# One-hot columns of a gather on TensorE: one wide compare of two tiles, or a compare per tile with a number per partition

## The reference

```python
for _ in range(2):                                   # the two passes that matter here
    edge_input = concatenate([h[src], h[dst], edge_attr_32], axis=-1)
    m_ij = relu(edge_input @ We1 + be1) @ We2 + be2
    h = h + segment_sum(m_ij, dst, num_segments=3125)
x = layernorm(x + (h + bias))
# third stage: out = segment_sum((x @ weight.T)[src] * norm, dst); relu; + x
x = layernorm(x + gcn(x))
```

## Time and profile before

| what | value |
|---|---|
| median of 3 runs | 2765.25 us (2763.64 to 2766.93) |
| profiled execution | 2764.02 us |
| its span, first to last instruction | 2762.2 us |
| TensorE (PE) busy | 2262.0 us, 82% |
| GpSimd (POOL) busy | 2012.3 us, 73% |
| VectorE (DVE) busy | 1467.6 us, 53% |
| ScalarE (ACT) busy | 703.4 us, 25% |
| mean granted TensorE clock | 0.882 |

### The profile page before, as it was taken

The page is one execution under the profiler, slowest core; times in us unless marked ns, Lnnn a source line. Parts: engine busy times, 40 slices in busy tenths (PEclk is TensorE's granted clock), DMA queues, the critical chain, the costliest instruction groups (busy, mean ns, idle before and its releaser), DMA issues.

```text
span 2762.2 us, 51738 instructions
## 1 busy us (share of the span) xinstructions
PE 2262.0 (82%) x15194; PEld 1711.8 (62%) x15384; DVE 1467.6 (53%) x3610; ACT 703.4 (25%) x1927; POOL 2012.3 (73%) x1765
## 2 busy tenths in 40 slices
PE   2798888888888888878788788888888868998986
PEld 2565656656566657555555555555555658888986
DVE  2755555554555554354444444444444368988885
ACT  2111111111111111111111111111111147877874
POOL 3677777777777777287887877777877737766763
PEclk8899999999989997589898999999898868999997
DMA  5333333333333334223333333333333321111111
GB/s 121 88 95 95 93 89 95 90 90 96 85 96 97 92 92 115 78 78 90 88 90 89 94 91 89 93 88 96 85 94 96 91 58 51 51 48 50 51 47 46
DMA packets 181877, 231.86 MB, mean 84 GB/s; under 512 B 75000, under 2 KB 133231, under 8 KB 181620
## 3 DMA queue, kind: packets, MB, share of 16 engines
q0 software_dynamic: 56000, 114.80, 15.7%
q1 hardware_dynamic: 118580, 111.47, 15.3%
q10 hardware_dynamic: 7168, 4.09, 0.5%
HBM read 220.06 MB, written 10.12 MB: 83 GB/s over the span
## 4 chain that ended last, share of the span: by engine, by line
POOL 47%; issue 31%; PE 10%; DVE 6%; DMA 3%; ACT 1%; DVEq 1%; POOLq 1%; SPq 0%; ACTq 0%
POOL gat L540 47%; PE ps L719 3%; PE ps L709 2%; PE ps L610 2%; DMA gat<-dst_row 1%; DVE msg L1282 1%; PE ps L797 1%; DVE khots L1277 1%; DMA gat<-z_dram,idx 1%; DMA cbase_dram<-cint 1%; PE ps L660 1%; DVE xTs L1279 1%; PE ps L793 1%; DMA dbc<-dst_row 1%; PE ps L628 0%
## 5 line engine op out<-in xcount | busy, mean ns | idle before, releaser
L540 POOL DMA_INDIRECT gat<-p_dram,idx x1422 | 1677.5, 1180 | 501.6 <-issue 430.8
L660 PE MATMUL ps<-node_a,x 128*128 128x512 bf16 x2210 | 779.7, 431 | 315.8 <-DVE node_a L1227 313.2
L660 PEld LDWEIGHTS ps<-node_a,x 128*128 128x128 bf16 x2400 | 247.2, 109 | 603.3 <-DVE node_a L1227 291.7
L1247 DVE TENSOR_TENSOR msg<-ps,gat 128x512 f32<-128x512 f32 (+1 forms) x404 | 250.9, 622 | 517.7 <-DMA gat<-p_dram,idx 500.4
L660 PE MATMUL ps<-node_a,adj 128*128 128x512 bf16 x1200 | 511.7, 426 | 0.0
L540 POOL DMA_INDIRECT gat<-z_dram,idx x328 | 322.0, 982 | 167.4 <-issue 98.3
L600 PEld LDWEIGHTS ps<-rhs,lhs 96*128 96x128 f32 x3232 | 408.2, 199 | 57.0 <-DVE lhs L1187 24.9
L600 PE MATMUL ps<-rhs,lhs 96*128 96x128 f32 x3232 | 412.0, 282 | 28.1 <-DMA rhs<-q_dram 21.8
L610 PE MATMUL ps<-hot,msg 128*128 128x64 f32 x3232 | 411.5, 282 | 12.8 <-ACT msg L902 12.8
L1187 DVE TENSOR_SCALAR lhs<-dbc,base_p 64x1024 f32<-64x1024 int32 x202 | 156.4, 774 | 486.1 <-DMA dbc<-dst_row 448.7
L610 PEld LDWEIGHTS ps<-hot,msg 128*128 128x128 f32 x3232 | 392.4, 198 | 20.9 <-ACT msg L902 14.3
(11 more groups left out here) (149 smaller groups left out, 1922.4 us busy)
## 6 DMA issues: line engine op xcount, KB each, us to landing
dbc<-dst_row SPq DMA_DIRECT2D x202, 256.0 KB
lhs<-eaT SPq DMA_DIRECT2D x202, 128.0 KB
gat<-p_dram,idx POOLq DMA_INDIRECT x1422
gatq<-src_row SPq DMA_DIRECT2D x48, 256.0 KB, 5.3
rhs<-q_dram SPq DMA_DIRECT2D x202, 32.0 KB
gat<-z_dram,idx POOLq DMA_INDIRECT x328
idx<-src_g SPq DMA_DIRECT2D x243, 4.0 KB
p_dram<-node_a ACTq DMA_DIRECT2D x12, 256.0 KB, 3.3
```

The lines of the kernel that those rows point to most:

```text
L540: return pool.indirect_dma_start(out=out_, out_offset=None, in_=table, in_offset=bass.IndirectOffsetOnAxis(ap=index, axis=0))
L660: mm = nc.tensor.matmul(ps_own, p_part[k][:, t, :], shot[j % 2][:, t - t0, :, :].rearrange("p j e -> p (j e)"), start=(t == 0 and k == 0), ...
L1247: V.tensor_tensor(msg[s][:, c0:c1, :], ps_pre(s, h)[:, 0:(c1 - c0) * P].rearrange("p (c f) -> p c f", f=P), gat[s][:, c0:c1, :], ALU.add). ...
```

## The change

The table `numbers` (25 tiles x 128 columns, f16, in which every column of a tile holds the same number) goes, and with it the two-operand compare. In its place stands `row_id`, one f32 number per partition and tile (128 x 25). A step's one-hot columns are made tile by tile: six or seven instructions of 4 x 128 columns, each with `sbc16` as its one SBUF operand and a column of `row_id` as the number to compare with. They stand at the same place of VectorE's program, and the last of them signals `shot_made`.

```diff
+        row_id = sb("row_id", [P, HI])
...
-        numbers = khots[:, :, :, :].rearrange("p s c k -> p (s c k)").bitcast(f16).rearrange("p (t e) -> p t e", t=HI)
...
-            pool.iota(numbers, pattern=[[P, HI], [0, P]], base=-MID, channel_multiplier=1,
+            pool.iota(row_id[:, :], pattern=[[P, HI]], base=-MID, channel_multiplier=1,
                       allow_small_or_imprecise_dtypes=True).then_inc(pool_const, 1)
...
                         t0, n = PARTS4[j]
-                        V.tensor_tensor(shot[j % 2][:, 0:n, :, :],
-                                        numbers[:, t0:t0 + n, :].unsqueeze(2).to_broadcast([P, n, 4, P]),
-                                        sbc16[:, :, :].unsqueeze(1).to_broadcast([P, n, 4, P]), ALU.is_equal
-                                        ).then_inc(shot_made, 1)
+                        for t in range(t0, t0 + n):
+                            last = V.tensor_scalar(shot[j % 2][:, t - t0, :, :], sbc16[:, :, :], row_id[:, t:t + 1],
+                                                   None, ALU.is_equal)
+                        last.then_inc(shot_made, 1)
```

## The result

| | before | after |
|---|---|---|
| median, same chip | 2764.44 us (2756.99 to 2766.93) | 2612.47 us (2609.7 to 2619.22, 4 runs) |
| profiled execution | 2764.02 us | 2609.70 us |
| mean granted TensorE clock | 0.882 | 0.903 |

The ratio is 0.9449, with a 95% interval of 0.9429 to 0.947 (in square brackets from here on). The change is worth 152 us where 233 were forecast, and the time lies 2.5 us above the range.

A forecast was written before the change was run, and what follows sets the result against it. The prediction took GpSimd's gathers, issued one after another, to bound the kernel. From 2764.0 us it took off 266 for the wide compare's holds and added 24 for L1187's and 9 for the chains': 2531 us, range 2495 to 2610.

The forecast's parts named there:

- What bounds the kernel: In both message passes GpSimd issues gathers one after another and waits for nobody; the passes cost what the gathers cost.
- The compares' own time: On VectorE, a short compare was to step every 0.27 us: six 1.6 us, seven 1.9 us, about as before.
- Half pace: Rivals with VectorE steps of 0.41 us: 2560 us with ways in (chance 0.05), 2915 us without (chance 0.05).
- So a one-operand instruction holds, but its end is a way in.: On VectorE, a gather held by a short one-operand instruction gets in at its end, so rows of them let gathers through.
- 192 chains give back 9 us: New holds by the short compares: 0.035 us per gather meeting a chain, 9 us in all, at most 85 us.
- about 1000: Sign in the profile after: the gathers' mean in both passes falls from 1160 and 1193 to about 1000 ns.
- No way in: Rival: the chain holds the gather to its end, some 0.1 us sooner than the wide compare; 2745 us, chance 0.03.
- L1187's own hold comes to light: 116 gathers begin in L1187; its own holds on them, 24 us, were counted inside the 266 us and remain.
- keeps its 39 us: L1085, another two-operand compare, was to go on holding gathers for 39 us, its place against them unmoved.
- TensorE: TensorE was to fit within GpSimd's 9.2 us step at 94%; the rival that it binds: 2575 us, chance 0.10.
- The waits for the compare: Sign in the profile after: TensorE's waits for the compare fall by half or more.
- The granted clock: Sign in the profile after: TensorE's granted clock rises over 0.93.

The follow-up runs named there:

- e12: The kernel before, with its wide two-operand compare moved ahead of L1187, nothing else changed: 2641.41 us, ratio 0.9557.
- e9: The changed kernel with the short compares moved ahead of L1187 in each step: 2510.29 us, ratio 0.9055.
- e13: The changed kernel with a memset of one partition and one column between L1187 and the first compare: 2510.1 us, ratio 0.9077.
- e5: The changed kernel with one one-operand compare for the whole step, all tiles compared with the first tile's number: 2599.96 us, one run.
- e6: The kernel before, with its wide two-operand compare cut into six or seven two-operand ones of 512 columns: 2740.37 us, ratio 0.9919.
- e1: The changed kernel with a semaphore increment ahead of each short compare: 2572.61 us, ratio 0.9304.
- e2: The changed kernel with one semaphore increment, between L1187 and the first compare only: 2573.49 us, ratio 0.9309.
- e4: The changed kernel with three one-operand compares a step, of two tiles each (the last three in seven-tile steps): 2614.55 us, one run.

## Why the prediction was wrong

**What bounds the kernel: right.** The profiled time less the gathers' busy time stays within 12 us over kernels that lie 255 us apart: 2764.0 - 1677.5 = 1086.5 before, 2609.7 - 1525.1 = 1084.6 after, 1084.3 with the wide compare ahead of L1187, 1092.1 with the short ones ahead, 1095.8 with the memset. Whatever a gather loses or wins, the kernel does.

**The compares' own time: right.** A step was to be 0.27 us and measured 0.262; six take 1.65 us (1.6 forecast) and seven 1.92 (1.9). Half pace is out.

**The failed step: "So a one-operand instruction holds, but its end is a way in."** I had read it at L1187 with L1222 behind it, and took it to hold for L1187 with a chain behind it. In 98 cases a gather that had come to L1187 wasn't let in there and paid for four or five compares besides. The term "192 chains give back 9 us" measured 124 us in its place. That is above its upper bound too, 85 us, since that let a gather pay for one compare and not for four. The pair in the earlier trace rows that would have warned me is the other one: with L1227 behind L1187 there was no way in, and I put that down to L1227's two operands alone. The place right behind L1187 had its part in it: with the wide compare ahead of L1187 (e12) the holds 0.82 us behind it are 127 us in place of 266. The third stage has only short instructions (0.24 to 0.30 us) in a row, none of 0.74 us with a chain right behind it; it could not show the case, and I let it speak for it.

That this step is the cause is shown by moving the chain (e9) or putting one tiny instruction ahead of it (e13). Both leave the chain's work as it is and take the 98 away, and both then run at 2510 us. In the memset version L1187's own hold at the first point is 25.5 us in 121 gathers (24 in 116 forecast), and what the chain holds is under 1 us, with some 6 more in 25 gathers that end behind the memset, which ends with L1187 (9 forecast). L1085's is 18 us (39). This last term is nearly the whole way from the forecast's 2531 us to the 2510 measured. The gathers' mean is 994 ns ("about 1000"), and two are over 1.7 us ("hardly one"). The rival *No way in* had the carry-over, but to the chain's end and for all 189, 2745 us. Half of it came true: 98 gathers, to two compares ahead of the end.

**L1187's and L1085's terms: too large.** "L1187's own hold comes to light", 24 us, came out at 9 us more than before (6 to 15), because gathers caught there were carried on. L1085 "keeps its 39 us" came out at 23. I had said that its place against the gathers doesn't move. Over the other kernels this term lies between 18 and 36 us, and no run shows what sets it. L1187's holds at the second point, which the prediction had no term for, fell by 6 us, as some of those gathers were carried on as well. Sum of what moved: -266 + 124 + 9 - 6 - 16 = -155, and some 3 us of small ones the other way, to the 152.4.

**TensorE: right that it isn't the bound.** Its waits for the compare are 187 us after the change, 127 in the memset version and 78 in e9, and these last two take the same time. The waits for the compare were to fall by half or more; they fell from 313 to 187 us, by two fifths, which was less than forecast. The granted clock was to be over 0.93 in the passes: it is 0.93 and 0.92. In the memset version it is 0.95 and 0.93.

**What a two-operand compare holds: half of it was misread.** The Trainium skill (SBUF — State Buffer, Who interferes with whom) says that a `tensor_tensor` takes only the read interface of the shared ports, and infers that it doesn't stall descriptor generation, which needs the write interface. The traces agree for a gather's second point. These are timelines of VectorE and GpSimd, of e12 (two operands) and then of e5 (one):

```profile
612.51 1.75 DVE L1227 TENSOR_TENSOR node_a<-khots,sbc 128x3072 bf16<-128x3072 f16 x1
612.43 0.97 POOL L540 DMA_INDIRECT gat<-p_dram,idx  x1 [0.30 <-issue]
...
600.47 1.04 DVE L1227 TENSOR_SCALAR node_a<-sbc,row_id 128x3072 bf16<-128x3072 f16 x1
600.52 1.11 POOL L540 DMA_INDIRECT gat<-p_dram,idx  x1 [0.30 <-issue]
```

The first gather comes to its second point at 613.25, with 1.0 us of the compare still to run, and ends at 613.40. The other would come to it at 601.34 and ends at 601.63, 0.12 us behind the compare's end at 601.51. Over both passes 35 gathers of the kernel before and 88 of e12 went through their second point within a running wide two-operand compare, and none was held there. Through the one-operand compare of 3072 columns none went, and 50 were held. The traces don't agree that a `tensor_tensor` doesn't stall the gathers at all: at their first point it holds them, moved (e12: 165 gathers, 127 us) or cut in tiles (e6) too. The prediction left out that the same section has a VectorE instruction with two SBUF inputs contend with a GpSimd instruction that reads SBUF. A gather takes its indices from `idx` in SBUF, so by that sentence the wide compare does cost something. That the first point is the reading of the indices would fit, but no run shows it.

The section's rule that a `tensor_scalar` in a two-port mode blocks GpSimd agrees with the 98 gathers held by the chain. It agrees with the 3584-column compare that held none if that one's slower pace (2.06 us against 1.04) means another mode; the runs show the pace alone.

**What stays open** is by what rule a passed-over gather gets in. Runs showed: two compares before the end of six and of seven; one before the end of three, and two where the last of the three has three tiles; at the end of a single one; one before the end of six and at the end of seven with two operands; and in steps of e1 and e2 one before the end of six and of seven. With nothing in between the way at L1187's end is mostly open in two kinds of step out of six, with an increment in four, other ones among them, with a memset in all. Why two steps with the same instructions differ is open too. That VectorE's queue hands out the chain before L1187 is over, and takes the port with it, would fit the first compare's unchanged start, but no run here shows the queue.

## What to carry to other kernels

A gather by indirect DMA can wait for the VectorE instruction that it meets and for several that stand directly behind it; read the end of each long gather against every VectorE instruction's end, less the rest of an undisturbed one (here 0.82 us, or 0.12 us for one held late), before an instruction is blamed. When a long instruction and a chain of short, quick instructions stand side by side, try a tiny instruction between them (here a memset of one element; a semaphore increment did two fifths of what that did), or let the chain come elsewhere in the step: here that was worth another 0.04 of the time, in one line. A way in that was seen behind one pair of instructions is a reading of that pair; for another neighbour it has a price of its own.

## What the runs showed of the hardware

- The hold goes both ways. With the memset, chains in which a gather gets in take 1.80 us instead of 1.65. The view of L1230's instructions from 595 to 598 us shows it (shortest, median and longest in ns):

```profile
L1230 DVE TENSOR_SCALAR node_a<-sbc,row_id x6: 330/340/473, 595.9 to 597.4; 128x512 bf16<-128x512 f16 x6
```

  One of the six takes 473 ns where the others take 330 to 344: it is the third, from 596.46 to 596.93, and the gather comes to its second point at 596.70. In the chain of the kernel after at 600.67, which passes the gather over, none is longer:

```profile
L1228 DVE TENSOR_SCALAR node_a<-sbc,row_id x6: 337/338/340, 600.7 to 602.0; 128x512 bf16<-128x512 f16 x6
```

  The Trainium skill (SBUF — State Buffer, Who interferes with whom) says that whoever issues first gets the port pair for the whole instruction. The trace agrees in that VectorE is made to wait too, by 0.13 us. It doesn't agree that GpSimd's gather holds it for its whole 0.94 us, as the five other compares run undelayed beside it.
- A one-operand compare of 3584 columns whose source is seven times the same 512 took 2.06 us, one of 3072 columns (six times) 1.04 us. In e4 a last piece of three tiles took 1.00 us against 0.48 for two. In the two cases at the lower pace the source repeats an odd number of times; the repeats of two and of six did not lose pace. These are the only cases tried.
- f16 in and bf16 out with a number per partition: 512 columns every 0.262 us, 256 columns every 0.20 us, so 256 more cost 0.06 us, 0.24 ns a column.
